# Second attention: q and k turned once per half batch, operands stacked through DRAM

## The chip, the core and the metric

One core of a Trainium2 chip runs the whole program. Its engines work side by side and meet by semaphores: TensorE (PE in the profile; its weight loads are PEld), VectorE (DVE), ScalarE (ACT), GpSimd (POOL) and SyncE (SP), which issues the DMAs. Each engine takes its instructions strictly in the order of the program. The metric is the device time of one execution in microseconds.

## The reference, cut

```python
def reference(x, ...):                                   # x: 8 sequences of 256 tokens, 256 features
    ...
    xn = _layernorm(x, axis=-1)
    s = _L1_attn_ref(xn, w_qkv, q_norm_w, k_norm_w, w_proj, b_proj)
    g = _silu(_L1_ffn_ref(xn, router_w, gate_w, up_w, down_w, ...))
    return x + s * g

def _L1_attn_ref(x, w_qkv, q_norm_w, k_norm_w, w_proj, b_proj):
    def rmsnorm(t, w):
        var = jnp.mean(t * t, axis=-1, keepdims=True)
        return t * jax.lax.rsqrt(var + EPS) * w
    B, L, dim = x.shape
    H = 16
    D = dim // H
    qkv = jnp.einsum('bld,ed->ble', x, w_qkv)
    qkv = qkv.reshape(B, L, 3, H, D).transpose(2, 0, 3, 1, 4)
    q, k, v = (qkv[0], qkv[1], qkv[2])
    q = rmsnorm(q, q_norm_w)
    k = rmsnorm(k, k_norm_w)
    scores = jnp.einsum('bhqd,bhkd->bhqk', q, k) * D ** (-0.5)
    attn = jax.nn.softmax(scores, axis=-1)
    out = jnp.einsum('bhqk,bhkd->bhqd', attn, v)
    out = out.transpose(0, 2, 1, 3).reshape(B, L, dim)
    return jnp.einsum('bld,ed->ble', out, w_proj) + b_proj
```

`_L1_ffn_ref` is a mixture of eight experts with two chosen per token, and a shared expert beside them. Ahead of this second layer stands a first one (an attention with 16 heads of 128 + 64 features and a quantized feed-forward part); the change doesn't touch it.

## The kernel before

The program has three stages; the last, `stage_layer1`, is the second layer, from about 890 us to the end. Products are made from 32-bit operands split into a high and a low part, so that a product is three matmuls (`product`, lines 58 to 60: high x high, high x low, low x high).

`stage_layer1` interleaves attention and experts. It runs over *slots* (`SLOTS`), one for each head of each of the 8 batches, n = 16 b + u, so u is the head; a run-up of 16 slots stands before slot 0, and 5 follow. On PE slot n consists of `scores(n + 1)` (two matmuls, line 1820, into the one score bank), the *jobs* and pieces of experts' work of the slot (`ITEMS[n]`), `turn(n - 1)` (four transposes of the normalised probabilities, line 1830) and `values(n - 2)` (four matmuls with V, line 1844). On the other engines a slot follows: VectorE takes the maximum (line 1680), ScalarE the exponentials (line 1465), VectorE the reciprocal, GpSimd the normalisation (line 1337), and ScalarE and VectorE the high and low part of the turned probabilities (lines 1473 and 1684). `turn(n)` waits for `turn_free`, which is VectorE's low part of the turn before.

Jobs write one of three PSUM banks (`PJ`), in turn; a job waits until the bank's former user is read out. For batch m: `T` transposes the normalised rows, `Q0`, `Q1` and `V` are the projections, `P0` and `P1` the output projection, `L` the router's logits, `C` the combine table. Experts come in 56 steps K (14 tiles of hidden features for each of 4 groups of 512 tokens); g, G, u, U are the halves of gate and up products, D0 and D1 those of the down product. A planner (`attn_jobs`, `COST`, `SLOT_GOAL`) puts the attention's jobs at fixed heads u and fills each slot with experts' pieces up to a goal in units of PE work: 10 units for scores, turn and values, 4 for a job of four transposes, 6 for each piece.

The part that the change replaces makes the score operands. A head has 16 features, and one matmul with 64 rows a head covers high x high, low x high, high x low and low x low at once; two heads, a *pair*, share the 128 partitions. q and k of a batch stand in `qk` with tokens on the partitions, scaled by `scale_rows` (DVE) and `weigh` (POOL). Then:

- ScalarE writes the high parts twice each into `stk` and `stq` (`k_hi`, `q_hi`, at u = 8, 9, 11, 12), VectorE the low parts of k (`k_lo`, line 1619), GpSimd those of q (`q_lo`);
- each pair has a job `S0` to `S7` at every second head, four slots ahead of its scores: PE transposes four 128x128 blocks of `stq` and `stk` (line 1773), ScalarE copies them to `zq` (two copies of 64 partitions, line 1420) and `sk` (line 1421), three buffers each (`NSTK`). `scores` waits until that job's bank is free.

SP issues the experts' loads in order of K: `load_gu` (gate and up weights, 512 KB, when `U` of K - 3 is done), `load_d` (down weights, when `D1` of three steps before is done), `store_combine` and `load_cb` (a DRAM copy of the combine table, broadcast to partitions; GpSimd multiplies it in at line 1344). Nothing else is on SP in this stage but the output's stores.

Of the kernel before, what the change touches and what calls it, by code (L numbers as in the profile page):

```python
# [6 lines left out]
F32 = mybir.dt.float32  # L7
# [1072 lines left out]
def stage_layer1(nc, sh, l1, wgu_dram, wd_dram, ct_dram, out):  # L1080
# [7 lines left out]
    UNIT, SLOT_GOAL, EARLY_GOAL = 10, 30.6, 14  # L1088

    def attn_jobs(n):  # L1090
# [42 lines left out]
    JOB = {item: i for i, item in enumerate(ORDER)}  # L1133
    U_AT = {n: [K for K in range(L) if AT["U", K] == n] for n in SLOTS}
# [32 lines left out]
    with ExitStack() as ctx:  # L1167
# [6 lines left out]
        stq, stk = n_.sb("stq", [P, TB, H1, 4, D1]), n_.sb("stk", [P, TB, H1, 4, D1])  # L1174
# [21 lines left out]
        gu_in = l1.gu_in  # L1196
        d_in, cb_in = ([n_.sem(f"{s}_in{i}") for i in range(3)] for s in ("d", "cb"))
# [3 lines left out]
            "sq_ready", "ms_ready", "newton", "scaled", "weighted", "k_hi", "q_hi", "k_lo", "q_lo",  # L1201
# [22 lines left out]

        def heads(t, part, half):

            at = part * D + half * P
            return qk[:, t, at:at + P].rearrange("p (h d) -> p h d", d=D1).unsqueeze(2).broadcast_to([P, 8, 2, D1])

        def half_of(rows, t, half):  # L1230
            return rows[:, t, 8 * half:8 * half + 8]
# [4 lines left out]
        with nc.Block() as block:  # L1236
            @block.sync
            def _(sp):
# [25 lines left out]

                def store(s):
# [8 lines left out]
                for K in range(L + 1):  # L1274
                    if 2 <= K < L:
                        load_gu(K)
# [13 lines left out]
            def _(pool):  # L1290
# [23 lines left out]

                def q_lo(m, half, t):
                    pool.wait_ge(S["q_hi"], 4 * m + 2 * half + t + 1)
                    pool.tensor_tensor(half_of(stq, t, half)[:, :, 1::2, :].bitcast(F32R), heads(t, 0, half),
                                       half_of(stq, t, half)[:, :, 0::2, :], ALU.subtract).then_inc(S["q_lo"], 1)
# [47 lines left out]
                for n in SLOTS:  # L1366
                    b, u = divmod(n, H1)
                    if b + 1 < BATCH:
# [4 lines left out]
                        if u in (9, 10, 13, 14):  # L1373
                            q_lo(b + 1, (u - 9) // 4, (u - 9) % 4)
# [20 lines left out]
            def _(act):  # L1395
                def job_out(item):
# [16 lines left out]
                    elif name[0] == "S":  # L1413
# [3 lines left out]
                        if pair >= NSTK:  # L1417
                            act.wait_ge(S["score_full"], 2 * (pair - NSTK) + 2)
# [564 lines left out]
```

## Time and profile before

| | us |
|---|---|
| median of 3 runs | 1409.71 (1409.17 to 1410.26) |
| profiled execution | 1408.91 |
| its span, first to last instruction | 1407.1 |
| PE busy in the span | 1368.9 (97%) |
| VectorE, ScalarE, GpSimd busy | 920.9, 820.0, 761.9 |

Busy time counts each engine's recorded instructions; a matmul's record begins at its start and reaches beyond the next one's start, so the distance between starts, not the length of a record, says how fast PE goes. Where a line ends with a bracket, the engine stood idle before it for so long, and the name in it is the instruction that it waited for.

### The profile page before, as it was taken

What the parts mean: (1) busy time and instruction counts of PE and PEld (TensorE: products, weight loads), DVE (VectorE), ACT (ScalarE), POOL (GpSimd) and SP (SyncE); (2) the same over time, 40 slices, a digit from 0 to 9 for tenths busy, and PEclk for the clock granted to TensorE, in tenths of its full rate; (3) what the DMA queues carried; (4) which work ended last, traced back from release to release, by engine and by line L of the source; (5) the groups of instructions that cost most, each with busy time, mean ns of one, the idle gap of its engine ahead of it and who ended that gap; (6) DMA issues with size and microseconds to landing.
All of it is one profiled execution on the core that took longest, in us unless ns stands there. A gap on an engine that the chain in (4) does not pass through costs nothing. (4 is left out here: it accounts for less than half of the span.)

```text
span 1407.1 us, 25856 instructions
## 1 busy us (share of the span) xinstructions
PE 1368.9 (97%) x8950; PEld 1221.1 (87%) x8950; DVE 920.9 (65%) x1793; ACT 820.0 (58%) x2172; POOL 761.9 (54%) x757
## 2 busy tenths in 40 slices
PE   9999899999999999999999999899999999999997
PEld 7887798999899989998999888788889888889887
DVE  6655566565656565656665665677777878777764
ACT  5553444554544555445544544378787788778873
POOL 2651433454434454435544443477669677777764
PEclk9999999999999999999999999999999999999999
DMA  5995333334332343223433334144233242342442
GB/s 197 323 330 198 85 91 89 92 80 120 100 94 52 101 130 99 75 75 98 114 86 94 113 75 165 68 122 150 83 98 123 68 150 84 120 120 92 143 122 90
DMA packets 85681, 165.64 MB, mean 118 GB/s; under 512 B 16720, under 2 KB 27664, under 8 KB 83248
## 3 DMA queue, kind: packets, MB, share of 16 engines
q1 hardware_dynamic: 85552, 163.99, 38.3%
q8 instruction: 73, 1.20, 0.4%
q14 instruction: 56, 0.46, 0.1%
HBM read 99.90 MB, written 22.09 MB: 87 GB/s over the span
## 5 line engine op out<-in xcount | busy, mean ns | idle before, releaser
L775 POOL TENSOR_TENSOR a_pr<-a_pr,a_ri 128x512 f32<-128x512 f32 x128 | 133.5, 1043 | 299.1 <-DVE a_ri L955 299.1
L832 ACT ACTIVATE a_pr<-a_score,a_nb 128x256 f32<-128x256 f32 x256 | 119.3, 471 | 266.3 <-DVE a_nb L947 266.3
L1337 POOL TENSOR_TENSOR l_pr<-l_pr,l_ri 128x512 f32<-128x512 f32 x128 | 133.5, 1043 | 119.0 <-DVE l_ri L1714 118.1
L1465 ACT ACTIVATE l_pr<-l_score,l_nb 128x256 f32<-128x256 f32 x256 | 119.2, 472 | 80.8 <-DVE l_nb L1680 80.2
L58 PE MATMUL a_job<-s_xs,s_wh 128*128 128x512 f32 x384 | 153.9, 401 | 1.0 <-PEq L221 1.0
L60 PE MATMUL a_job<-s_xs,s_wl 128*128 128x512 f32 x384 | 151.7, 395 | 0.0
L59 PE MATMUL a_job<-s_xs,s_wh 128*128 128x512 f32 x384 | 151.3, 394 | 0.0
L947 DVE TENSOR_REDUCE a_nb<-a_score 128x2 f32<-128x512 f32 x128 | 88.5, 692 | 85.0 <-PE a_score L1026 83.3
L1680 DVE TENSOR_REDUCE l_nb<-l_score 128x2 f32<-128x512 f32 x128 | 87.5, 684 | 34.0 <-PE l_score L1820 33.4
L960 DVE TENSOR_TENSOR a_pt<-a_turn,a_pt 128x512 fp32r<-128x512 f32 x128 | 87.5, 683 | 24.2 <-ACT a_pt L840 24.2
L1844 PE MATMUL l_out<-s_wh,l_vp 128*128 128x256 f32 x512 | 91.6, 300 | 0.9 <-DVE s_wh L1684 0.9
L58 PE MATMUL l_job<-l_xs,s_wl 128*128 128x512 f32 x224 | 90.6, 405 | 1.7 <-DVE l_ga L1594 1.7
L1684 DVE TENSOR_TENSOR s_wh<-l_turn,s_wh 128x512 fp32r<-128x512 f32 x128 | 87.2, 681 | 5.5 <-ACT s_wh L1473 5.4
L1473 ACT ACTIVATE s_wh<-l_turn 128x512 fp32r<-128x512 f32 x128 | 76.5, 597 | 23.4 <-PE l_turn L1830 23.0
L60 PE MATMUL l_job<-l_xs,s_wl 128*128 128x512 f32 x224 | 88.9, 397 | 0.0
L59 PE MATMUL l_job<-l_xs,s_wl 128*128 128x512 f32 x224 | 88.6, 396 | 0.0
L955 DVE RECIPROCAL a_ri<-a_sm 128x2 f32<-128x2 f32 x128 | 21.2, 166 | 102.3 <-ACT a_pr L832 102.3
L1830 PE MATMUL l_turn<-s_ident,l_pr 128*128 128x128 f32 x512 | 77.9, 275 | 10.5 <-DVE s_wh L1684 9.4
L60 PEld LDWEIGHTS a_job<-s_xs,s_wl 128*128 128x128 f32 x384 | 72.1, 188 | 16.9
L1830 PEld LDWEIGHTS l_turn<-s_ident,l_pr 128*128 128x128 f32 x512 | 59.3, 140 | 28.6 <-issue 13.6
L844 ACT ACTIVATE a_ot<-a_out 128x512 fp32r<-128x512 f32 x64 | 38.8, 606 | 77.8 <-PE a_out L60 76.8
L58 PEld LDWEIGHTS a_job<-s_xs,s_wh 128*128 128x128 f32 x384 | 72.2, 188 | 11.3 <-issue 1.4
(257 smaller groups left out, 4780.3 us busy)
## 6 DMA issues: line engine op xcount, KB each, us to landing
s_wl<-wgu_scratch SPq DMA_DIRECT2D x56, 512.0 KB, 4.8
a_sk<-a_rotk SPq DMA_DIRECT2D x384, 64.0 KB, 2.0
a_sq<-a_rotq SPq DMA_DIRECT2D x256, 64.0 KB, 2.0
s_xs<-xn_scratch SPq DMA_DIRECT2D x14, 1024.0 KB, 5.6
l_wd<-wd_scratch SPq DMA_DIRECT2D x56, 256.0 KB, 2.7
a_raw<-in_w SPq DMA_DIRECT2D x30, 256.0 KB, 3.0
wgu_scratch<-f_split SPq DMA_DIRECT2D x14, 512.0 KB, 4.7
f_praw<-in_moe_w SPq DMA_DIRECT2D x14, 384.0 KB, 4.5
```

The source lines that it names most:

```text
L58: pe.matmul(out, lh, rh, start=first, stop=False)
L59: pe.matmul(out, lh, rl, start=False, stop=False)
L60: return pe.matmul(out, ll, rh, start=False, stop=last)
L775: pool.tensor_tensor(e, e, ri[:, n % 2, :].unsqueeze(2).broadcast_to([P, 2, SEQ]), ALU.mult)\
L832: i = act.activation(pr[:, n % 2, t, :], PS[n % 2][:, t * SEQ:(t + 1) * SEQ], ACT.Exp, bias=nb[:, n % 2, t:t + 1], accum_out=sm[:, n % 2, ...
L947: dve.tensor_reduce(nb[:, (n + 1) % 2, :], PS[(n + 1) % 2][:, :].rearrange("p (t k) -> p t k", t=2), AX.X, ALU.max, negate=True).then_inc( ...
L960: dve.tensor_tensor(pt[:, n % 2, 1, :], PT[:, :], pt[:, n % 2, 0, :], ALU.subtract).then_inc(S["turn_free"], 1)
L1337: pool.tensor_tensor(e, e, ri[:, n % 3, :].unsqueeze(2).broadcast_to([P, 2, SEQ]), ALU.mult)\
L1465: i = act.activation(pr[:, n % 3, t, :], PS[n % NPS][:, t * SEQ:(t + 1) * SEQ], ACT.Exp, bias=nb[:, n % 3, t:t + 1], accum_out=sm[:, n % 3 ...
L1680: dve.tensor_reduce(nb[:, (n + 1) % 3, :], PS[(n + 1) % NPS][:, :].rearrange("p (t k) -> p t k", t=2), AX.X, ALU.max, negate=True).then_in ...
L1830: i = pe.transpose(PT[:, kc * SEQ + t * P:kc * SEQ + (t + 1) * P], pr[:, n % 3, t, kc * P:(kc + 1) * P], ident[:, :])
L1844: i = pe.matmul(PO[:, 0:SEQ], vp[:, kc, a, e * P:(e + 1) * P], pt[:, n % 2, q, kc * SEQ:(kc + 1) * SEQ], start=(e == 0 and kc == 0 and q = ...
```

## The change

q and k of a batch are no longer split and doubled before they are turned. Two jobs a batch, `X0` and `X1` (eight heads each, at u = 9 and 11 of the batch before), transpose the scaled rows of `qk` themselves, four blocks each. ScalarE copies the bank as the high part, VectorE subtracts for the low part, both into `tqk`. SP stores a half's high and low parts of q and k twice each into two scratch tensors in DRAM, in the order in which the score operands stack them (`store_stack`: eight stores of 128 KB, at u = 10 and 12), and loads each pair's operands back (`load_stack`: two loads of 64 KB and one of 128 KB, in every odd slot, five slots ahead). `scores` waits for these loads. `S0` to `S7`, `k_hi`, `q_hi`, `k_lo` and `q_lo` go. SP's program is now written by slots, with the experts' loads at the slots in which their buffers come free. The planner's goal falls from 30.6 to 29.1 units a slot.

```diff
-    UNIT, SLOT_GOAL, EARLY_GOAL = 10, 30.6, 14
+    UNIT, SLOT_GOAL, EARLY_GOAL = 10, 29.1, 14
...
-        m, r = divmod(n + 4, H1)
-        if r % 2 == 0 and 0 <= m < BATCH:
-            jobs.append((f"S{r // 2}", m))
+        if b + 1 < BATCH and u in (9, 11):
+            jobs.append((f"X{u // 2 - 4}", b + 1))
...
+    LOAD_SLOT, at = {}, SLOTS[0]
+    for K in range(L + 1):
+        s, k = divmod(K, MT)
+        at = max(at, AT["D1", K - 1 - ND] if K > ND else SLOTS[0], AT["C", s] if k == NSH + 1 and s < NSTEP else SLOTS[0])
+        LOAD_SLOT[K] = at
+    LOAD_GU = {K: AT["U", K - NGU] if K >= NGU else SLOTS[0] for K in range(L)}
...
-        stq, stk = n_.sb("stq", [P, TB, H1, 4, D1]), n_.sb("stk", [P, TB, H1, 4, D1])
+        tqk = n_.sb("tqk", [P, 2, 2, 2, SEQ], F32R)
...
+                def store_stack(m, half):
+                    wait_free(sp, (f"X{half}", m))
+                    heads = slice(8 * half, 8 * half + 8)
+                    for part, to, places in ((0, qs_dram, ((0, 2), (1, 3))), (1, ks_dram, ((0, 1), (2, 3)))):
+                        for low in range(2):
+                            for place in places[low]:
+                                sp.dma_start(to[m % 2, heads, place], tqk[:, half, low, part, :].bitcast(F32)).then_inc(tqk_out[half], 16)
+
+                def load_stack(pair):
+                    m, p = divmod(pair, H1 // 2)
+                    r = pair % NSTK
+                    if p % 4 == 0:
+                        sp.wait_ge(tqk_out[p // 4], 16 * 8 * (m + 1))
+                    if pair >= NSTK:
+                        sp.wait_ge(S["score_full"], 2 * (pair - NSTK) + 2)
+                    for h in range(2):
+                        sp.dma_start(zq[64 * h:64 * h + 64, r, h, :].bitcast(F32),
+                                     qs_dram[m % 2, 2 * p + h].rearrange("c d n -> (c d) n")).then_inc(zq_in[r], 16)
+                    sp.dma_start(sk[:, r, :].bitcast(F32), ks_dram[m % 2, 2 * p:2 * p + 2].rearrange("h c d n -> (h c d) n")).then_inc(sk_in[r], 16)
...
-                for K in range(L + 1):
-                    if 2 <= K < L:
-                        load_gu(K)
+                def load_experts(K):
                     if K >= 1:
                         load_d(K - 1)
...
+                for n in SLOTS:
+                    b, u = divmod(n, H1)
+                    if b + 1 < BATCH and u in (10, 12):
+                        store_stack(b + 1, u // 2 - 5)
+                    pair = (n + 5) // 2
+                    if n % 2 and 0 <= pair < N // 2:
+                        load_stack(pair)
+                    for K in LOAD_AT[n]:
+                        load_experts(K)
+                    for K in range(2, L):
+                        if LOAD_GU[K] == n:
+                            load_gu(K)
...
-                def q_lo(m, half, t):
...
-                    elif name[0] == "S":
-                        pair = m * (H1 // 2) + int(name[1])
-                        r = pair % NSTK
+                    elif name[0] == "X":
+                        half = int(name[1])
                         wait_full(act, item)
-                        if pair >= NSTK:
-                            act.wait_ge(S["score_full"], 2 * (pair - NSTK) + 2)
-                        for h in range(2):
-                            act.activation(zq[64 * h:64 * h + 64, r, h, :], bank[64 * h:64 * h + 64, 0:SEQ], ACT.Copy)
-                        act.activation(sk[:, r, :], bank[:, SEQ:2 * SEQ], ACT.Copy).then_inc(free_of(item), 1)
+                        if m >= 1:
+                            act.wait_ge(tqk_out[half], 16 * 8 * m)
+                        act.activation(tqk[:, half, 0].rearrange("p r n -> p (r n)"), bank[:, :], ACT.Copy).then_inc(S["turned_hi"], 1)
...
-                def k_hi(m, half):
...
-                def q_hi(m, half):
...
+                    elif name[0] == "X":
+                        half = int(name[1])
+                        dve.wait_ge(S["turned_hi"], 2 * m + half + 1)
+                        dve.tensor_tensor(tqk[:, half, 1].rearrange("p r n -> p (r n)"), bank[:, :],
+                                          tqk[:, half, 0].rearrange("p r n -> p (r n)"), ALU.subtract).then_inc(free_of(item), 1)
...
-                def k_lo(m, half):
...
-                    elif name[0] == "S":
-                        p = int(name[1])
-                        pe.wait_ge(S["q_lo"], 4 * m + 2 * (p // 4) + 2)
-                        pe.wait_ge(S["k_lo"], 4 * m + 2 * (p // 4) + 2)
-                        for k, rows in enumerate((stq, stk)):
+                    elif name[0] == "X":
+                        half = int(name[1])
+                        pe.wait_ge(S["weighted"], m + 1)
+                        for part in range(2):
                             for t in range(TB):
-                                i = pe.transpose(bank[:, k * SEQ + t * P:k * SEQ + (t + 1) * P],
-                                                 rows[:, t, 2 * p:2 * p + 2, :, :].rearrange("p h r d -> p (h r d)"), ident[:, :])
+                                at = part * D + half * P
+                                i = pe.transpose(bank[:, part * SEQ + t * P:part * SEQ + (t + 1) * P], qk[:, t, at:at + P], ident[:, :])
...
                     if u % 2 == 0:
-                        wait_free(pe, (f"S{u // 2}", m))
+                        pe.wait_ge(zq_in[r], 16 * 2 * (n // 2 // NSTK + 1))
+                        pe.wait_ge(sk_in[r], 16 * (n // 2 // NSTK + 1))
...
+    qs = nc.dram_tensor("qs_scratch", [2, H1, 4, D1, SEQ], F32, kind="Internal").ap()
+    ks = nc.dram_tensor("ks_scratch", [2, H1, 4, D1, SEQ], F32, kind="Internal").ap()
```

In the order of PE's instructions, slot 92 (batch 5, head 12), from its scores to its first down products. Before:

```order
L1820 MATMUL l_score<-l_sk,l_zq 128x256 x2
L58 MATMUL l_job<-l_xs,s_wl 128x512
L59 MATMUL l_job<-l_xs,s_wl 128x512
L60 MATMUL l_job<-l_xs,s_wl 128x512
L1773 MATMUL l_job<-s_ident,l_stq 128x128 x2
L1773 MATMUL l_job<-s_ident,l_stk 128x128 x2
L1742 MATMUL l_down<-l_wd,l_hid 128x256
L1743 MATMUL l_down<-l_wd,l_hid 128x256
L1744 MATMUL l_down<-l_wd,l_hid 128x256
```

Now (lines are numbered anew, 1816 are the scores, 1738 to 1740 the down products):

```order
L1816 MATMUL l_score<-l_sk,l_zq 128x256 x2
L58 MATMUL l_job<-l_xs,s_wl 128x512
L59 MATMUL l_job<-l_xs,s_wl 128x512
L60 MATMUL l_job<-l_xs,s_wl 128x512
L1738 MATMUL l_down<-l_wd,l_hid 128x256
L1739 MATMUL l_down<-l_wd,l_hid 128x256
L1740 MATMUL l_down<-l_wd,l_hid 128x256
```

The four transposes between the up product and the down product are gone; the rest of the slot is the same.

On ScalarE, slots 92 to 94: exponentials (1465, now 1470), turned probabilities (1473, now 1478), tanh of the gate (1442, now 1463), high part of the hidden features (1488, now 1493), output rows (1479, now 1484). Before:

```order
L1465 ACTIVATE l_pr,l_sm<-l_score,l_nb 128x256 x2
L1420 ACTIVATE l_zq<-l_job 64x256 x2
L1421 ACTIVATE l_sk<-l_job 128x256
L1473 ACTIVATE s_wh<-l_turn 128x512
L1465 ACTIVATE l_pr,l_sm<-l_score,l_nb 128x256 x2
L1442 ACTIVATE l_gt<-l_job 128x512
L1488 ACTIVATE l_hid<-l_ga 128x512
L1473 ACTIVATE s_wh<-l_turn 128x512
L1479 ACTIVATE l_ot<-l_out 128x256
```

Now:

```order
L1470 ACTIVATE l_pr,l_sm<-l_score,l_nb 128x256 x2
L1478 ACTIVATE s_wh<-l_turn 128x512
L1470 ACTIVATE l_pr,l_sm<-l_score,l_nb 128x256 x2
L1463 ACTIVATE l_gt<-l_job 128x512
L1493 ACTIVATE l_hid<-l_ga 128x512
L1478 ACTIVATE s_wh<-l_turn 128x512
L1484 ACTIVATE l_ot<-l_out 128x256
```

The three operand copies between the exponentials and the turned probabilities are gone.

On SP, the run-up: `l_wd` and `s_wl` are the experts' down and gate/up weights, `ct_scratch` and `l_cb` the combine table. Before:

```order
L1247 DMA l_wd<-wd_scratch 128x512
L1242 DMA s_wl<-wgu_scratch 128x1024
L1247 DMA l_wd<-wd_scratch 128x512
L1253 DMA ct_scratch<-l_ct 8x512
L1262 DMA l_cb<-ct_scratch 128x512
L1242 DMA s_wl<-wgu_scratch 128x1024
```

Now:

```order
L1242 DMA s_wl<-wgu_scratch 128x1024 x3
L1271 DMA qs_scratch<-l_tqk 8x16x256 x4
L1271 DMA ks_scratch<-l_tqk 8x16x256 x4
L1281 DMA l_zq<-qs_scratch 64x256 x2
L1283 DMA l_sk<-ks_scratch 128x256
L1271 DMA qs_scratch<-l_tqk 8x16x256 x4
L1271 DMA ks_scratch<-l_tqk 8x16x256 x4
L1247 DMA l_wd<-wd_scratch 128x512
L1253 DMA ct_scratch<-l_ct 8x512
L1262 DMA l_cb<-ct_scratch 128x512
L1242 DMA s_wl<-wgu_scratch 128x1024
L1281 DMA l_zq<-qs_scratch 64x256 x2
```

The stores and loads of the stacked operands stand between the experts' loads; the first store of a half waits for its `X` job, and line 1281's first load of a half waits until that half's eight stores have landed.

## Rows read from the trace of the kernel before

**Rows 1.** The page, part 1: busy us, share, instructions.

```profile
PE 1368.9 (97%) x8950; PEld 1221.1 (87%) x8950; DVE 920.9 (65%) x1793; ACT 820.0 (58%) x2172; POOL 761.9 (54%) x757
```

**Rows 2.** Busy us by stretch: PE, PEld, DVE, ACT, POOL, clock, DMA share, GB/s.

```profile
921.50:1391.40 469.90, 456.27 (x3185) 410.92 (x3186) 353.15 (x746) 362.20 (x1061) 344.99 (x418) 1.00 0.37 115
```

**Rows 3.** PE's timeline (start us, length us), slots 92, 93; last scores.

```profile
1261.14 0.39 PE L1820 MATMUL l_score<-l_sk,l_zq 128*128 128x256 f32 x2
...
1262.06 0.38 PE L1773 MATMUL l_job<-s_ident,l_stq 128*128 128x128 f32 x2
...
1262.42 0.37 PE L1742 MATMUL l_down<-l_wd,l_hid 128*128 128x256 f32 x1
...
1264.80 0.40 PE L1820 MATMUL l_score<-l_sk,l_zq 128*128 128x256 f32 x2
...
1268.04 0.40 PE L1820 MATMUL l_score<-l_sk,l_zq 128*128 128x256 f32 x2
...
1383.81 0.40 PE L1820 MATMUL l_score<-l_sk,l_zq 128*128 128x256 f32 x2
```

**Rows 4.** Groups by line: busy us, mean ns of one | idle before.

```profile
L1420 ACT ACTIVATE l_zq<-l_job 64x256 fp32r<-64x256 f32 x128 | 48.0, 375 | 1.5 <-PE l_job L1773 0.5
L1421 ACT ACTIVATE l_sk<-l_job 128x256 fp32r<-128x256 f32 x64 | 24.6, 385 | 0.7
L1773 PE MATMUL l_job<-s_ident,l_stq 128*128 128x128 f32 x128 | 24.4, 272 | 0.0
L1619 DVE TENSOR_TENSOR l_stk<-l_qk,l_stk 128x256 fp32r<-128x256 f32 x32 | 23.1, 762 | 0.0
```

**Rows 5.** Timeline of three engines in slots 26 to 28.

```profile
1017.90 0.76 ACT L1420 ACTIVATE l_zq<-l_job 64x256 fp32r<-64x256 f32 x2
...
1019.47 0.69 ACT L1438 ACTIVATE l_gz<-l_job,s_half_bias 128x512 f32<-128x512 f32 x1
...
1020.04 0.69 ACT L1439 ACTIVATE l_gt<-l_job,s_half_bias 128x512 f32<-128x512 f32 x1
...
1020.77 0.73 DVE L1582 SCALAR_TENSOR_TENSOR l_ga<-l_gt,l_gz 128x512 f32<-128x512 f32 x1 [2.57 <-ACT l_gt L1439]
...
1022.85 0.63 PE L1830 MATMUL l_turn<-s_ident,l_pr 128*128 128x128 f32 x4 [0.84 <-DVE s_wh L1684]
```

**Rows 6.** Waits in the stage: us in total, times, longest us.

```profile
DVE l_ga L1588 <- ACT l_gt L1442: 35.9, 36, 2.3
```

**Rows 7.** Timeline of the run-up: q weighted, second gate's tanh, first scores.

```profile
905.18 1.30 POOL L1312 TENSOR_TENSOR l_qk<-l_qk,s_nqk 128x512 f32<-128x512 f32 x1
...
910.48 0.68 ACT L1439 ACTIVATE l_gt<-l_job,s_half_bias 128x512 f32<-128x512 f32 x1
...
918.69 0.39 PE L1820 MATMUL l_score<-l_sk,l_zq 128*128 128x256 f32 x2
...
924.35 0.48 PE L1820 MATMUL l_score<-l_sk,l_zq 128*128 128x256 f32 x2
```

**Rows 8.** DMA issues on SP (ns min/median/max), one wait, landing us.

```profile
L1247 SPq DMA_DIRECT2D l_wd<-wd_scratch x56: 319/326/440, 889.9 to 1383.1; - x56
L689 SPq DMA_DIRECT2D a_sk<-a_rotk x384: 507/591/1725, 132.0 to 840.1; - x192
SPq L1262 <- DMA ct_scratch<-l_ct: 7.6, 4, 1.9
s_wl<-wgu_scratch SPq DMA_DIRECT2D x56, 512.0 KB, 4.8
xn_scratch<-s_xs SPq DMA_DIRECT2D x4, 1024.0 KB, 6.9
```

**Rows 9.** A combine row's load on SP, its line's landing, GpSimd's use.

```profile
1140.71 0.43 SPq L1262 DMA_DIRECT2D l_cb<-ct_scratch  x1
...
1146.19 1.29 POOL L1344 TENSOR_TENSOR l_ga<-l_ga,l_cb 128x512 f32<-128x512 f32 x1
...
DMA to landing us min/median/max: 2.3/3.6/4.5
```

More of the change, by code:

```diff
@@ L1077, in _, with stage_layer1 @@
                 rest(PS[(N - 2) % 2], 9)
-def stage_layer1(nc, sh, l1, wgu_dram, wd_dram, ct_dram, out):
+def stage_layer1(nc, sh, l1, wgu_dram, wd_dram, ct_dram, qs_dram, ks_dram, out):
     N = BATCH * H1
@@ L1133, in stage_layer1 @@
     JOB = {item: i for i, item in enumerate(ORDER)}
+    LOAD_SLOT, at = {}, SLOTS[0]
[4 more added lines that the diff above has]
+    LOAD_GU = {K: AT["U", K - NGU] if K >= NGU else SLOTS[0] for K in range(L)}
+    LOAD_AT = {n: [K for K in LOAD_SLOT if LOAD_SLOT[K] == n] for n in SLOTS}
     U_AT = {n: [K for K in range(L) if AT["U", K] == n] for n in SLOTS}
@@ L1196, in stage_layer1 @@
         gu_in = l1.gu_in
+        zq_in, sk_in = ([n_.sem(f"{s}_in{i}") for i in range(NSTK)] for s in ("zq", "sk"))
+        tqk_out = [n_.sem(f"tqk_out{i}") for i in range(2)]
         d_in, cb_in = ([n_.sem(f"{s}_in{i}") for i in range(3)] for s in ("d", "cb"))
@@ L1223, in tokens @@
             return slice(at, at + P)
[L1225 to L1231, printed above, removed]
         def wait_merged(engine, s):
@@ L1442, in job_out @@
                             act.activation(gt[:, m % 2, :], bank[:, :], ACT.Tanh, scale=0.5).then_inc(S["tanh_ready"], 1)
-                def k_hi(m, half):
-                    act.wait_ge(S["scaled"], m + 1)
-                    if m >= 1:
-                        wait_full(act, (f"S{4 * half + 3}", m - 1))
-                    for t in range(TB):
-                        act.activation(half_of(stk, t, half)[:, :, 0:2, :].bitcast(F32R), heads(t, 1, half), ACT.Copy)\
-                           .then_inc(S["k_hi"], 1)
-                def q_hi(m, half):
-                    act.wait_ge(S["weighted"], m + 1)
-                    if m >= 1:
-                        wait_full(act, (f"S{4 * half + 3}", m - 1))
-                    for t in range(TB):
-                        act.activation(half_of(stq, t, half)[:, :, 0::2, :].bitcast(F32R), heads(t, 0, half), ACT.Copy)\
-                           .then_inc(S["q_hi"], 1)
                 def exps(n):
@@ L1614, in scale_rows @@
                                       rq[:, :].unsqueeze(2).broadcast_to([P, 4 * H1, D1]), ALU.mult).then_inc(S["scaled"], 1)
-                def k_lo(m, half):
-                    for t in range(TB):
-                        dve.wait_ge(S["k_hi"], 4 * m + 2 * half + t + 1)
-                        dve.tensor_tensor(half_of(stk, t, half)[:, :, 2:4, :].bitcast(F32R), heads(t, 1, half),
-                                          half_of(stk, t, half)[:, :, 0:2, :], ALU.subtract).then_inc(S["k_lo"], 1)
                 def rows(ap):
@@ L1884, in program @@
             stage_attention0(nc, a, sh, s0, l1, xn0, g0, w1, wp, wgu)
-        stage_layer1(nc, sh, l1, wgu, wd, ct, out)
+        stage_layer1(nc, sh, l1, wgu, wd, ct, qs, ks, out)
 def tile_weights(gate, up, down):
```

17 lines of the change are left out of this document (2 added, 15 removed).

## The prediction

> **What bounds the kernel now.** First the busy shares of the page: TensorE is busy 97% of the span, the next engine 65% [rows 1]. A share over two attention stages says little about the stage that changes, so I cut that stage out by its own marks. Its main loop has 128 slots, one a head; a slot begins with the two score matmuls of the next head (L1820). The loop's first slot begins at 921.5 us and its last ends at 1391.4: 469.9 us, in which PE is busy 456.3 us (97%), VectorE 353.2, ScalarE 362.2, GpSimd 345.0 at a granted clock of 1.00, the upper level of 2.4 GHz [rows 2]. So PE's own instructions are the first suspect. The view that decides is PE's timeline of two neighbouring slots. Slot 92 holds one stacking job (four transposes, L1773) beside six 512-column and six 256-column products, slot 93 the same without the job: 1261.14 to 1264.80 = 3.66 us, and 3.24 us [rows 3]. The difference, 0.42 us, is the job. A slot without a wait is as long as PE's instructions, so an instruction taken from PE shortens the program.
>
> That holds for most slots, not all. I priced every slot from 1 to 125 by its jobs at such undisturbed spacings and compared it with the distance between the score rows (128 of them, 918.69 to 1383.81 [rows 3, 7]). About 20 us are left over, in some 30 slots. The 51 slots planned at 22 units average 0.12 us over their work, the 32 at 18 units 0.32 us. One of them shows what waits: in slot 27 ScalarE copies the stacked operands (from 1017.90), therefore comes late to the gate (1019.47, 1020.04), VectorE stands idle for 2.57 us until that is done, and PE then stands 0.84 us before its next transposes until VectorE has subtracted [rows 5]. In the whole stage VectorE idles 35.9 us for the routed experts' tanh on ScalarE [rows 6].
>
> **The change part by part.**
>
> *PE.* Eight stacking jobs a batch become two jobs of the same four 128x128 transposes; 8 batches x 6 = 48 jobs go. In the run-up to slot 0 two go and two come, so all 48 leave the loop. By the neighbouring slots a job costs 0.42 us, by the starts inside slot 92 (1262.06 to the next products, whose first is stretched) 0.44; I take 0.43: **48 x 0.43 = 20.6 us** off PE. The new plan's goal of 29.1 units a slot instead of 30.6 is lower by just the 1.5 units that leave, so experts' products stay spread over the same slots, and most slots become 18-unit ones (85 instead of 33).
>
> The recorded duration of one transpose is 0.27 us [rows 4], but the records overlap: two together take 0.38 [rows 3]. The Trainium skill (TensorE: Matmul & The Clock Gate, Part 4: PE-mode transpose) gives about 275 ns for one in a kernel; 192 of those would be 53 us. The distance between slots says 20.6, and I go by it.
>
> *ScalarE.* The operand copies go (48.0 + 24.6 = 72.6 us [rows 4]) and, with them, the 64 copies of the high parts. Sixteen 128x512 copies out of PSUM come, at 0.7 us by a 128x512 row (0.68 [rows 7]): 11 us. *VectorE* loses 23.1 us of low parts [rows 4] and gets 16 subtractions of about 0.7 us (0.73 [rows 5]): net -12. *GpSimd* loses its 32 low parts. All three are beside PE's work, so none of it counts directly; it counts through the 20 us of stalls. The cover they give PE rises: ScalarE frees more than 61 us in the stage, some 0.5 us a slot, where a slot shrinks by 0.16. Stalls of the kind in rows 5 should mostly go. Against it stands that an 18-unit slot leaves PE's transposes only some 0.5 us behind VectorE's pair of 0.7 us operations, where a 22-unit slot left 0.9. Bounds: +10 us (85 slots at the old 18-unit mean of 0.32 and 11 at 0.12, with the rest as now, are 30 us instead of 20) to -10 us (half of the stalls go). I take **-3**: nearer to the gain because the engine that was late in the rows is the one relieved.
>
> *The way through DRAM, in the run-up.* Here nothing hides it. Batch 0's q is weighted by 905.18 + 1.30 = 906.5 [rows 7]; PE can turn it then. ScalarE reaches the first turned half only behind the tanh that ends at 911.1 [rows 7], copies it by 911.8 and VectorE subtracts by 912.5. Then SP issues eight stores. An issue took 0.33 us for a plain load and 0.59 for one that gathers partitions [rows 8]: 2.6 to 4.7 us. The wait for a store to DRAM was 7.6/4 = 1.9 us for 16 KB; 1 MB in one piece landed in 6.9 us [rows 8]; I take 2.3 behind the last issue, so 4.9 to 7.0 in all. Then three loads, 1.0 to 1.8 us of issue and 2.3 to land. The first scores can start at 920.7 to 923.6; now they start at 918.69 [rows 7]. Behind these loads SP issues the other half's eight stores, a weight load, the combine table's store and the 1.9 us wait for it, a table load and a weight load (3.4 us), and only then the second pair's loads. Pair 1 lands at 927.8 to 933.4, and its first scores, at 924.35 now [rows 7], start 3.4 to 9.1 us later. Some 1 us of it covers a stall that slot 1 has now. **+2.4 to +8; I take +5.5.**
>
> The Trainium skill (DMA: Bandwidth & Descriptors, Anatomy of one DMA) puts a DMA at 2.0 us plus its bytes at 436 GB/s: an estimate of 4.4 us for the eight stores' 1 MB, with which the run-up would lose some 1 to 3 us less. Its section Rules for kernel authors speaks against the change: many small transfers are better made one large one. No row here has a store of this shape.
>
> *The way through DRAM, in the loop.* A batch adds 16 stores and 24 loads, 13 to 24 us of SP's issue in some 56 us. A half is turned in slots 9 and 11, stored in 10 and 12, its first pair loaded from slot 11, and used by scores in slot 15: four slots (14 us) for about 10. I cost this at nothing. What hides it is the lead; if it is gone, PE waits before scores, in order, and everything with it. Queued behind the stores and behind the wait for them on SP are the experts' weights. These are asked for 10 us late at most, land 4.8 us after their issue [rows 8], and their three buffers leave about one slot still. The tightest is the combine row: it is issued at 1140.71, lands 3.6 us later and is used at 1146.19 [rows 9], 1.9 us to spare. In batches 3 and 4 the stores stand before such a load; worked out slot by slot it comes up to 4 us late three times, on GpSimd, which has most of two slots before PE asks for its result. **+0.5, at most +5.**
>
> *Sum* against the profiled execution, 1408.9 us (span 1407.1): 1408.9 - 20.6 - 3 + 5.5 + 0.5 = 1391.3. The median of the runs shown, 1409.7, lies 0.8 above it: **1392 us**.
>
> **The rivals.**
> - *The chain over VectorE sets the slot* as soon as PE's part is 3.24 us: for it, the 0.32 us of the 18-unit slots; against it, VectorE's 2.8 us a slot, and ScalarE as the cause in rows 5 and 6. Half or all of the +10, with the run-up at its upper end: 1397 to 1407, middle 1402. Chance 0.24.
> - *ScalarE's relief removes the stalls* (-10) and the run-up costs 3: 1380 to 1386. Chance 0.10.
> - *Slower: SP is held by its own wait for the stores.* If stores of 1 KB rows to DRAM take not 2.3 but 9 us to be seen, each wait holds the experts' weights 6.7 us more, 3.3 beyond the slot that they have to spare: 7 batches x 3.3 = 23, and the run-up 6.7 more: about 1422. It decides from about 8 us on, where a batch loses more than the 2.6 us that it saves. Against it: 1.9 us seen, and 6.9 for 1 MB with its data. Chance 0.04.
> - *Nothing gained*: stalls take all that PE frees, 1407 to 1412. The equal pair of slots speaks against it. Chance 0.04.
> - *Transposes cost their recorded 0.27 us*: 192 x 0.27 = 52 us, about 1361. Rows 3 deny it. Chance 0.01.
>
> **How the numbers follow.** The forecast, 1386 to 1397, has 0.57. From 1385 to 1403 lie the forecast, most of the first rival and the top of the second: 0.8. Measurements of this kernel agree within about 0.2% (2.8 us). Faster by more than that needs less than 1406.9: 0.57 + 0.10 + 0.01 and most of 0.24, 0.91. Within 0.2%: 0.05. Slower: 0.04.
>
> **What would show it.** PE's matmul count falls by 192 and the jobs of four transposes are 16; undisturbed slots of 18 units stay at 3.24 us; the loop from first score to last value is 446 us or so; VectorE's waits for ScalarE's tanh fall well below 35.9 us; the first scores start at 920 to 924. Wrong would be: many slots over 3.5 us, PE waiting for a DMA before scores inside the loop, or for expert weights; a lower granted clock in a stretch where PE waits in the run-up.

## The result: 3% slower, and where the time went

The changed kernel takes **1453.35 us** (median of 6 runs, 1449.64 to 1455.08) against 1409.47 for the kernel before: a ratio of **1.0302** (95% interval 1.0290 to 1.0314). The forecast was 1392, in a range up to 1403. The profiled execution took 1452.56 us with a span of 1450.3. Its engine shares, beside [rows 1]:

```profile
span 1450.3 us, 25396 instructions
PE 1361.8 (94%) x8758; PEld 1214.0 (84%) x8758; DVE 906.6 (63%) x1777; ACT 746.7 (51%) x1932; POOL 737.3 (51%) x725
PEclk9999999999999999999999999799999999999999
```

192 transposes are gone (8950 to 8758 matmuls) and ScalarE has 73 us less to do, and yet PE's share fell from 97% to 94%: PE waits. The page's chain that ended last now holds a queue that was not in it before, SP's, and the combine table's transfers:

```profile
PE 15%; DVE 7%; DMA 4%; SPq 4%; POOL 3%; issue 2%; ACT 2%; ACTq 0%; POOLq 0%; DVEq 0%
```

To place the loss I cut the stage at the starts of the score rows. From the stage's beginning to the start of slot 2 the changed kernel loses 18.1 us (slot 2 begins at 946.68, before at 928.55). Behind the last scores both take the same (23.3 us). Slots 2 to 125 are these two stretches; the columns are those of [rows 2]: length, busy us of PE, PEld, DVE, ACT, POOL, granted clock, DMA share, GB/s. First the kernel before:

```profile
928.55:1383.81 455.26, 443.25 (x3108) 399.54 (x3106) 344.28 (x727) 353.95 (x1037) 335.56 (x411) 1.00 0.37 114
```

and the changed one:

```profile
946.68:1426.95 480.27, 431.44 (x2919) 387.92 (x2917) 330.80 (x711) 285.18 (x811) 313.35 (x382) 0.97 0.57 171
```

PE's busy time fell by 11.8 us, while its idle time rose from 455.26 - 443.25 = 12.0 to 48.8 us. PE's busy time does not fall by the forecast's 20 because the clock fell as well: 0.97 instead of 1.00 (a mended kernel below, `e9_all_table`, with the same products at 1.00, is busy 423.9, so the lower clock costs 7.6). So: -19.4 for the transposes, +7.6 clock, +36.8 idle = +25.0 here, and +18.1 before it: 43.1 of the span's 43.2.

Who waits for what says the rest. Waits in the stage, its run-up included (us in total, times, longest), changed kernel; GpSimd had no wait of the first kind before:

```profile
POOL l_ga L1370 <- DMA l_cb<-ct_scratch: 47.7, 11, 8.0
PE l_turn L1826 <- DVE s_wh L1682: 43.3, 24, 8.8
PE l_score L1816 <- DMA l_sk<-ks_scratch: 13.8, 2, 8.4
PE l_down L1738 <- DVE l_y L1660: 4.7, 2, 4.0
```

Two of these belong to the run-up: both waits for the operands (`l_sk`), and the longest for the combine row, 8.0 us. From slot 2 on GpSimd waits ten times for the row, 39.7 us in all, at most 6.8. PE's longest wait, in slot 112, followed along the chain (start us, us, what; rows of pure issue time left out):

```profile
1366.88 0.89 SPq L1271
...
1367.81 0.68 SPq L1281
...
1369.18 0.58 SPq L1283
...
1369.80 0.43 SPq L1247
...
1370.28 0.43 SPq L1262
...
1370.75 5.41 DMA l_cb<-ct_scratch
...
1376.29 1.27 POOL l_ga L1370
...
1377.58 0.02 ACT l_hid L1493
...
1378.12 0.59 ACT l_gt L1463
...
1378.73 0.69 DVE l_ga L1592
1379.42 0.60 DVE l_nb L1678
1380.02 0.61 DVE s_wh L1682
...
1380.76 1.09 PE l_turn L1826 x4
```

Read it from the top: SP ends the last store of a half (L1271), issues a pair's operands (L1281, L1283) and a down weight (L1247), and only then the combine row (L1262). GpSimd multiplies by it at 1376.29. ScalarE's next instruction in order is the copy of that product (L1493), behind it stands the next gate's tanh (L1463), which VectorE waits for with the softmax's maximum and the turned probabilities behind it, and PE's next transposes need those. PE stands 8.83 us. And then it runs slowly:

```profile
1372.00:1380.76 8.76, 0.00 (x0) 0.03 (x1) 1.89 (x3) 2.31 (x6) 4.47 (x6) 0.62 0.96 293
1381.00:1384.00 3.00, 3.00 (x16) 3.00 (x16) 1.60 (x4) 0.78 (x3) 2.70 (x3) 0.50 0.35 109
1384.00:1386.50 2.50, 2.50 (x15) 2.19 (x15) 0.62 (x2) 2.02 (x7) 1.31 (x2) 0.91 0.41 97
```

After the idle stretch the granted clock is 0.50, the lower level of 1.2 GHz, for the 3 us shown: four transposes take 1.09 us, where rows of the same line at full clock have 0.60 to 0.63.

### The profile page after: what moved, and what is told of

It is laid out like the page before. It is cut to its first block and busy times, and to the rows that moved or that the text cites. A ratio compares the mean times of both kernels' runs of the same rounds, so it can differ in the third digit from the quotient of the medians.

```text
span 1450.3 us, 25396 instructions
## 1 busy us (share of the span) xinstructions
PE 1361.8 (94%) x8758; PEld 1214.0 (84%) x8758; DVE 906.6 (63%) x1777; ACT 746.7 (51%) x1932; POOL 737.3 (51%) x725
## 5 line engine op out<-in xcount | busy, mean ns | idle before, releaser
L1678 DVE TENSOR_REDUCE l_nb<-l_score 128x2 f32<-128x512 f32 x128 | 87.5, 683 | 40.5 <-PE l_score L1816 40.1
L1370 POOL TENSOR_TENSOR l_ga<-l_ga,l_cb 128x512 f32<-128x512 f32 x44 | 56.9, 1292 | 47.7 <-DMA l_cb<-ct_scratch 47.7
```

Source lines behind the costliest of these rows:

```text
L1678: dve.tensor_reduce(nb[:, (n + 1) % 3, :], PS[(n + 1) % NPS][:, :].rearrange("p (t k) -> p t k", t=2), AX.X, ALU.max, negate=True).then_in ...
```

## The experiments

Theory A, from the chain: on SP's queue the stores, the wait for them and the operand loads stand ahead of the combine row; a late row stops GpSimd, ScalarE, VectorE and PE in turn, because each works in order. Rival B: the DMA engines' load (0.57 instead of 0.37) makes every transfer late. In the changed kernel slots 62, 79, 96 and 112 take 9.41, 9.58, 8.36 and 13.53 us, where the same slots took 4.33, 3.58, 3.67 and 3.69 before; I name these four below.

### What of SP's work makes the row late

`e3_no_stores` leaves out the stores behind batch 0 and the waits for them; the operand loads stay and read batch 0's rows:

```
...
-                    if b + 1 < BATCH and u in (10, 12):
+                    if b + 1 == 0 and u in (10, 12):
                         store_stack(b + 1, u // 2 - 5)
...
```

> The changed kernel without the stores of batches 1 to 7 and the waits for them (batch 0's stay); all operand loads stay and read batch 0's rows, so the output is wrong. Theory A with the stores and their wait as what holds SP (5.1 us of issue and 3 to 4.4 us of waiting a half): the same stalls go as with early combine rows, about 43 us; time 1410 us (1402 to 1418), GpSimd's wait for the combine row under 8 us. Rival A2 (the operand loads alone, 1.7 us before each weight, make the row late): the waits stay over 25 us and the time over 1430. Rival B (full DMA engines): the 16.8 MB of stores are half of what came in, so about half of the 43 us goes: about 1430.

Measured: **1413.94 us**; slots 62, 79, 96, 112 at 4.34, 3.24, 3.23, 3.77; GpSimd's wait 8.6 us, one wait, in the run-up. Slots 2 to 125:

```profile
945.88:1388.04 442.16, 424.44 (x2920) 381.69 (x2918) 331.96 (x713) 284.39 (x811) 314.15 (x382) 0.99 0.51 153
```

`e4_no_loads` leaves out the operand loads from pair 3 on and keeps the stores and the wait for them; the scores go on with the first pairs' operands:

```
                     if pair >= NSTK:
-                        sp.wait_ge(S["score_full"], 2 * (pair - NSTK) + 2)
+                        return
...
```

> The changed kernel without the operand loads from pair 3 on (the scores go on with the pairs of the first loads, so the output is wrong); all stores and the waits for them stay. Theory A with the stores and their wait as the holder: GpSimd's waits for the combine row stay above half of 47.7 us; time 1420 to 1440 us. Rival A2 (the operand loads make the row late): waits under 10 us, time 1405 to 1415. Rival B: as the stores, about half, 1430.

Measured: **1435.87 us**, GpSimd's wait 33.1 us in 12. So leaving out the stores and their wait saves 39 us, and taking 1.7 us of operand issue from each pair saves 17. In slots 2 to 125 alone the first saves 38.1 (480.27 to 442.16) and the second 12.0 (to 468.25, in a profiled run that is the slowest of its four); the best kernel below (`e9_all_table`) is 40.5 shorter there. 38.1 and 12.0 are together more than that: both kinds of work stand in the same queue, and their costs don't add. That is what a queue with a lead would do: nothing is lost until the lead is used up, everything beyond is.

`e1_cb_early` leaves all of SP's work in place and asks for the combine rows two experts' steps earlier, into five buffers:

```
-    NJ, NPS, NSTK, NGU, ND, NCB, NHID = 3, 1, 3, 3, 3, 3, 3
+    NJ, NPS, NSTK, NGU, ND, NCB, NHID = 3, 1, 3, 3, 3, 5, 3
...
+                    if k > NSH + 1 and k + 1 < MT:
+                        load_cb(K + 1)
                     if K >= 1:
                         load_d(K - 1)
...
-                    if K >= 1 and not is_shared(K - 1):
-                        load_cb(K - 1)
+                        for ahead in range(3):
+                            load_cb(K - 1 + ahead)
```

> The changed kernel with one thing moved: the combine rows are asked for two experts earlier (five buffers instead of three), ahead of the down weights; stores and operand loads stay where they are. Theory A (on SP the stores, the wait for them and the operand loads stand before the combine rows; GpSimd then waits in order, behind it ScalarE, VectorE, PE): the slots 17, 48, 49, 62, 63, 77, 79, 80, 96, 97, 112, 113, which are together about 43 us over their undisturbed length, come back to within 5 us of it; GpSimd's waits for the combine row fall from 47.7 us to under 5; the run-up pays up to 2 us more. Time about 1412 us (1405 to 1420). Rival B (it is the DMA engines' load that makes every transfer late, 0.57 busy instead of 0.37): asking earlier moves the wait to the next late transfer, expert weights or operands; over 1430.

Measured: **1424.36 us**, 29 us less, not 41. GpSimd's wait fell to 9.3 us, of which 7.8 are the first row in the run-up; from slot 2 on it is 1.5, as expected. But now something else is late behind the same stores, the operands and gate weights themselves:

```profile
PE l_score L1818 <- DMA l_sk<-ks_scratch: 20.1, 7, 10.5
PE l_turn L1828 <- DVE s_wh L1684: 12.3, 21, 1.6
PE l_down L1740 <- DVE l_y L1662: 4.7, 2, 4.0
PE l_job L58 <- DMA s_wl<-wgu_scratch: 4.2, 2, 3.0
```

Five of the seven waits for operands, 5.6 us, stand in slots 2 to 125, where the changed kernel had none. The order on SP is the cause by A, but asking for one victim earlier is only part of a cure; what holds the queue has to become shorter.

### What makes a store hold SP so long

`e5_four_stores` writes the two copies of each row block with one store (the scratch's rows go from place-major to row-major, for q and k alike):

```
...
-                            for place in places[low]:
-                                sp.dma_start(to[m % 2, heads, place], tqk[:, half, low, part, :].bitcast(F32)).then_inc(tqk_out[half], 16)
+                            rows = tqk[:, half, low, part, :].bitcast(F32).unsqueeze(1).broadcast_to([P, 2, SEQ])
+                            sp.dma_start(to[:, low], rows).then_inc(tqk_out[half], 16)
...
-    qs = nc.dram_tensor("qs_scratch", [2, H1, 4, D1, SEQ], F32, kind="Internal").ap()
+    qs = nc.dram_tensor("qs_scratch", [2, H1, D1, 4, SEQ], F32, kind="Internal").ap()
```

> The changed kernel with four stores a half instead of eight: each store writes its rows to both places (the scratch has its rows in another order, the same for q and k); bytes, waits and all else are the same. Theory A (SP's time before the combine row is what counts; issue of the stores is 5.1 us of the 8.5 to 9.5 us that a half holds SP): issue falls to about 2.5 us a half, the seven large stalls lose 2 to 2.5 us each, the run-up 2.5 before the first score and 2.5 before score 2: 1433 us (1427 to 1440). Rival (the wait for the data in DRAM alone counts, or an issue's time grows with its bytes): 1449 or more.

Measured: **1415.88 us**: a gain of 37, nearly twice the 20 that I expected. Either the wait is far more than proportional, or the row order that came along did it. Two runs on that:

`e10_six_stores` keeps q's broadcast store and writes k singly, in the new row order:

```
...
+                    for low in range(2):
+                        for r in range(2):
+                            sp.dma_start(k[:, low, r], tqk[:, half, low, 1, :].bitcast(F32)).then_inc(tqk_out[half], 16)
...
```

> The changed kernel with six stores a half: q's rows written to both places by one store, k's singly; bytes and waits are the same. It lies between eight (1453.4 us) and four (1415.9 us). Theory A with a slack (SP is late only by what its work between a half's stores and the combine row exceeds the lead of that row): the wait is more than proportional above some number, so six lie nearer to four: 1420 to 1432 us. Rival (each store costs its issue, linear): 1434.6 us; rival (the wait for the data): 1450.

Measured: **1414.12 us**, below the range and no worse than four. So not the number. `e11_eight_layout` has eight stores, and the row order alone changed:

```
...
-                            for place in places[low]:
-                                sp.dma_start(to[m % 2, heads, place], tqk[:, half, low, part, :].bitcast(F32)).then_inc(tqk_out[half], 16)
+                            for r in range(2):
+                                sp.dma_start(to[:, low, r], tqk[:, half, low, part, :].bitcast(F32)).then_inc(tqk_out[half], 16)
...
```

A store's rows in the scratch were 8 heads x 16 rows x 256 numbers, with a gap behind each head; now they are 128 x 256 with one stride.

> The changed kernel with eight stores a half as before, but the scratch's rows in the order of the six- and four-store kernels, so that a store's 128 rows have one stride (128 x 256 instead of 8 x 16 x 256); number, bytes and waits are the same. It tells number and row order apart, since six stores gave what four gave. Theory A (the number of issues, with a slack): issue stays 5 us a half, time 1440 to 1454 us, GpSimd's wait for the combine row over 30 us. Rival O (the order of the rows makes the issue or the landing shorter): the issue of one falls from 0.6 to about 0.4 us or the wait behind a half's stores from 3.5 to about 2, time 1412 to 1430.

Measured: **1419.45 us**. With the same number of stores and the same bytes, 34 of the 44 us are gone: rival O holds. My theory that the issues' number counts falls for these 34; at most the 4 to 5 us between this run and the two before it are left to the number. The store's rows (issue time ns min/median/max), changed kernel:

```profile
L1271 SPq DMA_DIRECT2D qs_scratch<-l_tqk x64: 570/612/869, 913.3 to 1364.2; - x64
L1271 SPq DMA_DIRECT2D ks_scratch<-l_tqk x64: 570/571/1518, 916.0 to 1366.9; - x64
```

and with rows of one stride, eight stores:

```profile
L1273 SPq DMA_DIRECT2D qs_scratch<-l_tqk x64: 320/433/629, 913.6 to 1333.5; - x64
L1273 SPq DMA_DIRECT2D ks_scratch<-l_tqk x64: 432/452/1492, 915.6 to 1335.6; - x64
```

Both parts of the hold shrink. The hold is the issue of a half's stores and, behind a first half, the time from the end of the last store to the first operand load that waits for them (in five of the eight batches SP issues a few other loads in it). From the timeline of SP, medians over the batches, in us; GpSimd's wait is that of the whole stage:

| kernel | issue of a half's stores | wait behind a first half | hold | GpSimd's wait for the row | slots 2 to 125 | time |
|---|---|---|---|---|---|---|
| changed, eight | 5.3 | 3.5 | 8.8 | 47.7 | 480.3 | 1453.4 |
| e11, eight, one stride | 3.9 | 2.4 | 6.3 | 19.0 | 453.7 | 1419.5 |
| e10, six | 3.9 | 2.2 | 6.1 | 13.4 | 448.5 | 1414.1 |
| e5, four | 2.6 | 3.2 | 5.8 | 11.4 | 446.6 | 1415.9 |
| e3, none behind batch 0 | 0 | 0 | 0 | 8.6 | 442.2 | 1413.9 |

In slots 2 to 125 the 2.5 us of hold between 6.3 and 8.8 cost 26.6 us; the 6.3 below cost 11.6. (The times differ by less, 1413.9 to 1419.5, because e3 keeps the slow stores of batch 0 in the run-up: its slot 2 begins at 945.88, that of e11 at 941.11.) Why one stride is quicker: in the run-up, while the second half's stores fly alone, the changed kernel's DMA share stays at 0.52, and that of e11 is 0.81 (columns as above; first the changed kernel, then e11):

```profile
926.60:929.50 2.90, 2.90 (x11) 2.61 (x12) 1.45 (x3) 1.02 (x4) 0.03 (x1) 0.50 0.52 168
```

```profile
925.00:926.50 1.50, 1.50 (x11) 1.36 (x10) 1.38 (x2) 0.68 (x3) 0.00 (x0) 1.00 0.81 273
```

The Trainium skill (DMA: Bandwidth & Descriptors, Rules for kernel authors, the row on using all 16 engines) says that a DMA runs on at most as many engines as the size of its slowest dimension allows; 8 x 16 x 256 would keep a store to eight of the sixteen. The share of 0.52 fits that, and it is the rule that I should have weighed before. No run here tells the engines' number and the addresses in DRAM apart, so the mechanism stays argued; that the row order is the cause is shown. It also bears against B: e11's DMA share in slots 2 to 125 is 0.60, higher than the changed kernel's, at 34 us less.

### The run-up, slot 104, and all of it together

`e2_pairs_first`: in the run-up the loads of pairs 0 to 2 go ahead of the second half's stores and the combine table.

```
+                    if n == -5:
+                        for ahead in range(NSTK):
+                            load_stack(ahead)
-                    if n % 2 and 0 <= pair < N // 2:
+                    if n % 2 and NSTK <= pair < N // 2:
```

> The changed kernel with the loads of the first three operand pairs put ahead of the second half's eight stores and of the combine table's wait, in the run-up only. Theory A on the run-up (score 2 waits because pair 1's loads stand behind those on SP): slot 0 falls from 10.83 us to about 3.5, slot 1 as before; time about 1445 us (1442 to 1448), first scores unchanged at 926.5 or up to 1 us later. Rival (pair 1 is late because the DMA engines are full): slot 0 stays over 8 us and the time over 1450.

Measured: **1454.89 us**, no gain, though slot 0 fell from 10.83 to 2.54 us as theory A said. Slot 1 rose from 5.11 to 13.89: the first combine row now came last, GpSimd's longest wait for it is 12.0 us, and the maximum of the next scores stood behind it. One wait in the place of another, at about the same price.

`e6_sum_slot`: in slot 104 `D0.42` behind the up products instead of ahead of them.

```
+            if ("D0", MT * s) in ITEMS[n] and ("D1", MT * s - 1) in ITEMS[n - 1]:
+                ITEMS[n] = [x for x in ITEMS[n] if x != ("D0", MT * s)] + [("D0", MT * s)]
```

> The changed kernel with one product moved: in slot 104 the first down product of step 3 goes behind the two up products instead of ahead of them; nothing else changes. Theory Y (in slot 104 PE reaches that product before VectorE has read the down banks of the step before, 4.0 us of PE's wait; the new plan made that): slot 104 falls from 8.81 us to about 5, time 1449 us (1446 to 1451). Rival (the wait only moves to the product's new place or to the gate): 1452 to 1454.

Measured: **1448.12 us** (1445.77 to 1450.56), slot 104 at 7.21 instead of 8.81. The time is as expected, but the slot gave only 1.6 us of the 3.8 expected: PE's wait there fell from 4.0 to 2.6 us. The profiled run (1450.11) is 2.4 us below the changed kernel's, so the rest of the 5.2 us between the medians is not shown to come from this move. The wait itself is for VectorE's reading of the down banks, not for a DMA. Both plans have `D0.42` in slot 104; the new one puts it first, where a gate product and a stacking job stood ahead of it before and PE waited 0.9 us.

`e7_all` joins early rows, four stores, e6's move and e2's, with the second half of batch 0 stored only in slot 0:

```
...
-                    if b + 1 < BATCH and u in (10, 12):
+                    if b + 1 < BATCH and u in (10, 12) and n != 12 - H1:
                         store_stack(b + 1, u // 2 - 5)
+                    if n == 0:
+                        store_stack(0, 1)
...
```

> The changed kernel with all of it: combine rows two experts earlier, four stores a half, slot 104's product moved, and in the run-up the loads of pairs 0 to 2 ahead of the combine table with the second half of batch 0 stored only in slot 0. Theory A with the forecast's own sum for PE (48 jobs of 0.43 us fewer): first scores at 923 to 924, slots 0 to 2 together about 11 us (17.2 us less the slot-1 wait that the combine table then makes), slots 2 to 125 about 437 to 443 us: 1396 to 1406 us, below the kernel before. Rival B (full DMA engines, or a loop bound by VectorE's chain at 3.5 us a slot): loop above 450, time above 1410.

Measured: **1405.48 us**, 0.9962 of the kernel before (0.9948 to 0.9975), at the upper end of what I expected: slots 2 to 125 are within it, but the first score comes at 925.43, and slots 1 and 2 take 6.96 and 5.58 us, again for the first combine row. `e8_all_192` puts 192 transposes back on it:

```
+                    if u % 2 == 0 and u // 2 not in (3, 7):
+                        for t in range(4):
+                            pe.transpose(PS[n % NPS][:, t * P:(t + 1) * P], ident[:, :], ident[:, :])
```

> The mended kernel (combine rows early, four stores, slot 104, run-up) with 192 transposes put back on PE: four of the identity into the score bank, ahead of the scores of six even heads of each batch; nobody reads them. It prices what the change took off PE. Forecast's step: 48 x 0.43 = 20.6 us above the mended kernel (15 to 24, less if waits cover some). Rivals: recorded length, 192 x 0.27 = 52 us; PE not the bound of the loop, 0 to 5 us.

Measured: **1415.83 us**, 10.35 more, half of what I expected. Slots 2 to 125, first e7, then e8:

```profile
938.66:1379.51 440.85, 424.05 (x2917) 381.55 (x2917) 333.05 (x713) 285.27 (x812) 314.13 (x382) 0.99 0.60 190
```

```profile
940.09:1394.28 454.19, 443.82 (x3100) 404.77 (x3101) 333.05 (x713) 285.76 (x812) 314.33 (x382) 0.99 0.59 184
```

PE's busy time rises by 19.8 us for the 46 jobs in there, 0.43 each: the price is right. But PE's idle time falls by 6.4 (16.8 to 10.4), 6.0 of it in its waits for VectorE's low part of the turn (13.1 to 7.1), so 13.3 arrive in these slots. The profiled run of e8 is the slowest of its seven (1412.40 to 1419.42); by the medians 10.35 arrive. So a third to a half of what comes off PE goes into waits, most of them for VectorE.

`e9_all_table` is e7 with the combine table stored, and its first rows asked for, while SP would only wait for the first stores; and `D0.42` (with it `D0.14`) one slot later.

```
...
                     if n == -5:
-                        for ahead in range(NSTK):
-                            load_stack(ahead)
+                        store_combine(0)
+                        load_cb(NSH)
+                        load_stack(0)
+                        load_stack(1)
+                        load_cb(NSH + 1)
+                        load_cb(NSH + 2)
+                        load_stack(2)
```

> The mended kernel once more, with two places of order changed: the combine table is stored and its first rows asked for while SP would only wait for the first stores of q and k, ahead of the operand loads; and the first down product of a step stands one slot later where it would meet VectorE's reading of the down banks. Theory (the 6.96 and 5.58 us of slots 1 and 2 are the first combine row's lateness, the 6.1 us of slot 104 PE's wait for that reading): slots 1 and 2 come to 4.2 and 3.6 us, slot 104 to 3.3 and slot 105 one us longer; 1398 to 1401 us. Rival (the waits are only handed on to the operands of pair 1 and to VectorE): 1404 to 1406, as the mended kernel was.

Measured: **1398.34 us**, 0.9915 of the kernel before (0.9901 to 0.9930): 0.85% less than before the change. Slot 1 fell to 3.78 us and slot 2 to 3.50, as expected; slot 104 kept 5.25 (3.3 expected) and slot 105 takes 4.77, so there the wait was only handed on. Its slots 2 to 125:

```profile
932.90:1372.68 439.78, 423.88 (x2916) 381.36 (x2917) 332.14 (x713) 284.70 (x812) 314.43 (x382) 1.00 0.61 191
```

The DMA share is 0.61, the highest of these stretches, in the fastest kernel, and the combine row's median from issue to landing is 3.6 us in the changed kernel as in the one before. So rival B is out as the engines' mean load. A part of it stays: the longest landing rose from 4.5 to 6.9 us, and in slot 112, where the transfers behind the held queue are issued together, the share is 0.96 and the row takes 5.41. What this burst adds to a hold was not tested by itself.

## Why the prediction was wrong, step by step

In slots 2 to 125 the transposes gave -19.4 us, the stalls that e9 keeps +3.9, and what e9 wins back +40.5 (SP's hold, the clock behind it and a little of slot 104); ahead of them stands the run-up's +18.1. Together they are the 43.1 us found above. Forecast were -20.6, -3, +0.5 and +5.5.

- **PE, -20.6: right.** At the same clock PE's busy time in slots 2 to 125 falls from 443.25 to 423.88 us (e9): 19.4 for the 47 jobs that leave there, 0.41 each; put back, 0.43 (e8). Slots of 18 units without a wait stay at 3.23 to 3.25 us. The rival that takes the recorded 0.27 us of a transpose as its price is refuted.
- **Stalls, -3: wrong in sign, by little.** With SP out of the way PE's idle time is 15.9 us (e9) against 12.0, +4 instead of -3. ScalarE's relief did not do what I read from [rows 5, 6]: VectorE's waits for tanh hardly move, and PE's waits for VectorE grow. In the loop of the kernel before, and then of e9:

```profile
DVE l_ga L1588 <- ACT l_gt L1442: 34.4, 35, 2.3
...
PE l_turn L1830 <- DVE s_wh L1684: 9.4, 14, 1.3
```

```profile
DVE l_ga L1611 <- ACT l_gt L1482: 32.9, 34, 1.8
...
PE l_turn L1845 <- DVE s_wh L1701: 14.4, 20, 2.1
```

  Slot 27 itself did heal (4.29 to 3.68 us), but PE now waits 1.15 and 1.30 us in slots 54 and 67, where it did not; the new plan puts less of PE's work into them. Some 2 us of e9's waits are slot 104's. This is the first rival, the chain over VectorE, just below the lower end of its price (+5).
- **Run-up, +5.5 (2.4 to 8): missed, +18.1.** The stores began at 913.3, as computed (912.5). Then "4.9 to 7.0 in all" for eight stores and their landing was 9.5: I had taken 0.33 to 0.59 us an issue from [rows 8] and 2.3 behind the last; they were 0.57 to 0.61 with outliers above 1, and 3.4. The 4.4 us that the prediction estimates from the Trainium skill (DMA: Bandwidth & Descriptors, Anatomy of one DMA) are further off; that page measured its formula on DMAs issued from GpSimd, and these stores are issued from SP. The first scores came at 926.54, 3 us past my range. Pair 1 was to start by 933.4 and started at 941.57: the second half's eight stores, the table's wait and a 5.2 us landing stand before it. With four stores in the quicker row order and another order on SP the run-up costs 4.35 (e9: slot 2 begins at 932.90).
- **The loop's way through DRAM, +0.5 at most +5: the step that failed.** "I cost this at nothing. What hides it is the lead" and "it comes up to 4 us late three times, on GpSimd, which has most of two slots before PE asks for its result". From slot 2 on the row came up to 6.8 us late, ten times, in all batches from 0 to 7 but one (batch 2) and not only in batches 3 and 4; without the stores these slots take 38.1 us less (e3), so the term that I put at 0.5 measures about 38. What I had looked at held: the operands' lead of four slots was enough, and PE never waited for them from slot 2 on. What failed is the lead of the row behind the hold, and GpSimd's slack was the wrong cover: I followed the product to PE's down products, which I gave two slots, and not to the next instruction in order on ScalarE, the copy L1493. ScalarE waited 52.0 us for that product (2.7 before):

```profile
L1370 POOL TENSOR_TENSOR l_ga<-l_ga,l_cb x44: 1260/1296/1316, 938.5 to 1432.7; 128x512 f32<-128x512 f32 x44
...
  ACT l_hid L1493: 52.0, 22
```

- **The rivals.** "SP is held by its own wait for the stores" had the right place and 0.04. I tied it to one number, 9 us until a store is seen, and that number is 3.5; but the hold is issue plus wait, 8.8 us, and the first victim is not the experts' weights, with one slot to spare, but the combine row with 1.9 us [rows 9]. Had I put the threshold on the sum of all that stands in the queue, against the smallest lead behind it, I would have given it a higher chance.
- **The clock** was named as a danger in the run-up alone; in the loop it cost 7.6 us, behind the long waits.

## What to carry to other kernels

A step that is moved to a queue costs nothing only if issue plus waiting, in one piece, is shorter than the smallest lead of anything queued behind it; look for that one, and follow its wait through each engine's next instruction in order, not through the data alone. Above the lead the loss is steep (here 2.5 us more of hold cost 27 us over seven batches), so a small change of a transfer's shape can decide. When a wait is taken away, look which one was second: early rows showed the next and pairs first only exchanged one for another.

## What the runs showed of the hardware that I had not expected

- The same 128 KB store from 128 partitions to DRAM took 0.57 to 0.61 us to issue as 8 x 16 rows and 0.43 to 0.45 as 128 rows of one stride (medians), and a half's eight were seen 3.5 against 2.4 us after the last issue. With such stores alone in flight the DMA share was 0.52 in the first shape.
- One store that writes its rows to two places (256 KB) issues in 0.60 to 0.64 us, so four of them take 2.6 us where eight single ones take 3.9; but they land later (median 3.8 us after issue, against 2.6), and the hold is almost the same, 5.8 and 6.3.
- Four transposes between products cost PE 0.41 to 0.43 us, though the record of each is 0.27 us long.
